# Path entries compared on GpSimd instead of rectified twice on ScalarE, and the sums of places of the alignment begun before both comparisons are done

## The reference, cut to what matters

```python
x = x + _L0_xattn_ref(ctx_1024, _layernorm(x), ...)
x = x + _L0_ffn_ref(_layernorm(x), ...)
x = x + _L1_xattn_ref(ctx_1024, _layernorm(x))     # alignment
x = x + _L1_ffn_ref(_layernorm(x), ...)            # conv block

def _align_one(small, large):                      # per sequence
    D = _pairwise_euclidean(small, large)          # 128 x 128
    R = _dtw_cost(D)                               # r = d + min(up, left, diag)
    i_idx, j_idx, valid = _backtrack(R, T_small, T_large)
    contrib = small[i_idx] * valid[:, None]
    return jnp.zeros((T_large, d)).at[j_idx].add(contrib)

def _L1_ffn_ref(x, w1, conv_w, conv_b, w2):        # bit_linear quantises x and w
    h = bit_linear(x, w1)                          # 256 -> 1024
    h = depthwise_conv1d(h, conv_w, conv_b)        # three taps over the tokens
    h = jax.nn.silu(h)
    return bit_linear(h, w2)                       # 1024 -> 256
```

## Time and profile before

| | |
|---|---|
| median of 3 runs | 3391.78 us (3389.9 to 3393.14) |
| the profiled execution | 3391.26 us, of which 3389.5 us from the first to the last instruction |
| mean granted TensorE clock | 0.956 of full speed |
| busy over the span | PE 91%, DVE 72%, ACT 53%, POOL 38% |
| the alignment's last turn (the scan waits for TensorE) to its first step back | 2888.0 to 2895.3 us |
| start of the convolution to its first hidden tile | 2957 to 2993 us |
| convolution, steps | 2993 to 3389 us |

### The profile page before, as it was taken

One profiled execution on the slowest core, in us unless ns is written; L12 is line 12 of the kernel. 1 busy time (PEld: TensorE's weight loads), 2 busy tenths in 40 slices (PEclk: granted clock), 3 DMA queues, 4 the chain that ended last, 5 costly groups with the idle time before them and its releaser, 6 DMA issues. The chain is left out here.

```text
span 3389.5 us, 63898 instructions
## 1 busy us (share of the span) xinstructions
PE 3082.9 (91%) x23092; PEld 2669.3 (79%) x23092; DVE 2443.4 (72%) x5410; ACT 1787.2 (53%) x4638; POOL 1296.7 (38%) x1194
## 2 busy tenths in 40 slices
PE   6999999999999999999998999999999953158887
PEld 5888888888888888888887888888888841046665
DVE  5666666666666666666666787878787759769998
ACT  5565655555555555555554333333333326179996
POOL 2333333333333333333332333333333320058886
PEclk9999999999999999999999999999999975589999
DMA  5000000000000000000001112121212151011101
GB/s 159 5 8 5 8 5 8 5 7 5 8 5 8 5 8 5 8 5 8 4 5 57 58 51 64 51 66 50 65 54 61 58 80 42 1 31 38 50 32 38
DMA packets 108535, 103.81 MB, mean 31 GB/s; under 512 B 26560, under 2 KB 87488, under 8 KB 108224
## 3 DMA queue, kind: packets, MB, share of 16 engines
q1 hardware_dynamic: 108224, 99.72, 10.2%
HBM read 86.55 MB, written 13.14 MB: 29 GB/s over the span
## 5 line engine op out<-in xcount | busy, mean ns | idle before, releaser
L794 POOL TENSOR_TENSOR attention_prob<-attention_prob,attention_inv_sums 128x1024 f32<-128x1024 f32 x256 | 479.6, 1894 | 399.8 <-DVE attention_inv_sums L652 399.8
L504 ACT ACTIVATE attention_prob<-attention_turns,attention_neg_max 128x256 f32<-128x256 f32 x1024 | 467.6, 482 | 175.3 <-DVE attention_neg_max L643 175.3
L1371 POOL TENSOR_TENSOR experts_hidden_lo<-experts_weighed,experts_hidden_hi 128x512 fp32r<-128x512 f32 x192 | 255.0, 1328 | 531.4 <-ACT experts_hidden_hi L1124 531.4
L659 DVE COPY attention_probT<-attention_turns 128x512 f32<-128x512 f32 x512 | 329.0, 684 | 163.1 <-PE attention_turns L380 163.0
L346 PE MATMUL attention_turns<-kv_hi,wkv 128*128 128x512 f32 x1024 | 374.1, 406 | 0.0
L643 DVE TENSOR_REDUCE attention_neg_max<-attention_turns 128x2 f32<-128x512 f32 x512 | 318.1, 684 | 45.2 <-PE attention_turns L370 44.3
L1124 ACT ACTIVATE experts_hidden_hi<-experts_weighed 128x512 fp32r<-128x512 f32 x192 | 121.4, 632 | 404.1 <-DVE experts_weighed L1261 404.1
L314 PE MATMUL attention_turns<-wkv,kv_hi 128*128 128x512 f32 x1024 | 329.8, 403 | 2.1 <-DVE kv_lo L677 2.1
L495 ACT COPY attention_v<-attention_turns 128x512 f32<-128x512 f32 x256 | 149.9, 585 | 311.1 <-PE attention_turns L314 311.1
L380 PEld LDWEIGHTS attention_turns<-ident,attention_prob 128*128 128x128 f32 x2048 | 240.0, 141 | 36.6 <-POOL attention_prob L794 3.2
L380 PE MATMUL attention_turns<-ident,attention_prob 128*128 128x128 f32 x2048 | 265.9, 273 | 2.8 <-POOL attention_prob L794 2.8
(11 more groups left out here) (287 smaller groups left out, 8948.1 us busy)
## 6 DMA issues: line engine op xcount, KB each, us to landing
experts_spread<-shares SPq DMA_DIRECT2D x256, 128.0 KB, 3.0
attention_ctx<-in_ctx SPq DMA_DIRECT2D x32, 256.0 KB, 2.7
experts_far_ctxT<-in_ctxT SPq DMA_DIRECT2D x32, 256.0 KB, 3.6
weights_ctx<-in_ctx SPq DMA_DIRECT2D x16, 512.0 KB, 3.9
out<-conv_x_out SPq DMA_DIRECT2D x15, 512.0 KB, 2.9
x_all<-in_x SPq DMA_DIRECT2D x7, 1024.0 KB, 9.2
first_x<-norms SPq DMA_DIRECT2D x16, 256.0 KB, 3.1
dist<-experts_far SPq DMA_DIRECT2D x16, 256.0 KB, 2.5
```

Source lines behind the costliest of these rows:

```text
L504: made = act.activation(prob[n % 2][:, h, :], bank_of("s", 2 * n + e)[:, m * 256:(m + 1) * 256], ACT.Exp, bias=neg_max[:, n % 2, 2 * e + m ...
L659: dve.tensor_copy(probT[n % 2][:, 2 * g:2 * g + 2].rearrange("p h t c -> p (h t c)"), bank_of("t", 2 * n + g)[:, :]).then_inc(p_copied, 1)
L794: pool.tensor_tensor(prob[n % 2][:, :, :], prob[n % 2][:, :, :], inv[:, n % 2, :].unsqueeze(2).broadcast_to([P, QH, 2 * TOK]), ALU.mult).t ...
L1371: pool.tensor_tensor(hid_lo[n % 3][:, :], weighed[n % 2], hid_hi[n % 3][:, :].bitcast(F32), ALU.subtract).then_inc(hid_split, 1)
```

## The change: the second and third pass of a path become one comparison on GpSimd, and the last turn of the alignment is reordered

Convolution. `path_gap` and ScalarE's `path_entry` are gone. GpSimd has a `path_entry` of four `tensor_scalar` comparisons (distance <= reach, 128x128 f32, per-partition scalar), at m = 4 for group g+3. Its `finish` moves from m = 1 and 3 to m = 2 and 6. `middles` makes the reach with its other sign. The first three groups' paths are made on GpSimd too, that of group 2 after the two first `inverse_std` and ahead of the steps.

Alignment. `gather` begins with the two `places` products, which wait for no comparison, then adds the `falls` of both banks (after `falls` alone is made: new semaphore `fallen`), then `left`, bank 1 first. For the last chunk the scan is cut in two, bank 1 first, and `differ` waits for each half by itself.

```diff
-                pe.wait_ge(compared, c + 1)
                 if c:
                     pe.wait_ge(scanned, c)
                 for b in range(2):
                     pe.matmul(entry_ps[:, b, :], plus[:, :], places[:, :, :].rearrange("p r j -> p (r j)"),
                               start=True, stop=False, skip_group_check=True)
-                    for weight, flags in ((minus_far, left), (minus_half, falls)):
+                for weight, flags, ready in ((minus_half, falls, fallen), (minus_far, left, compared)):
+                    pe.wait_ge(ready, c + 1)
+                    for b in reversed(range(2)):
...
             def differ(c):
-                pe.wait_ge(scanned, c + 1)
                 if c:
                     pe.wait_ge(risen, 2 * c)
                 for b in reversed(range(2)):
+                    pe.wait_ge(scanned, c + 1 + (c == CHUNKS - 1 and not b))
...
-                dve.tensor_tensor_scan(entered[:, :, :].rearrange("p r j -> p (r j)"),
-                                       goes_on[:, :, :, :].rearrange("p b r j -> p (b r j)"),
-                                       entry_ps[:, :, :].rearrange("p b n -> p (b n)"), 0.0, ALU.mult, ALU.max
-                                       ).then_inc(scanned, 1)
+                for r in (slice(0, 2 * HC),) if c < CHUNKS - 1 else (slice(HC, 2 * HC), slice(0, HC)):
+                    cols = slice(r.start * N, r.stop * N)
+                    dve.tensor_tensor_scan(entered[:, r, :].rearrange("p r j -> p (r j)"),
+                                           goes_on[:, :, :, :].rearrange("p b r j -> p (b r j)")[:, cols],
+                                           entry_ps[:, :, :].rearrange("p b n -> p (b n)")[:, cols], 0.0,
+                                           ALU.mult, ALU.max).then_inc(scanned, 1)
...
-            def path_gap(g, rows=range(GB), step=None):
-                s = g % 2
-                act.wait_ge(distance_made, g + 2 if step is None else step)
-                for i in rows:
-                    made = act.activation(gap[s][:, i, :], gap[s][:, i, :], ACT.Relu,
-                                          bias=neg_reach[:, GB * g + i:GB * g + i + 1])
-                made.then_inc(gap_made, 1)
-
-            def path_entry(g, rows=slice(0, GB), step=None):
-                s = g % 2
-                act.wait_ge(gap_made, g + 2 if step is None else step)
-                if g >= 2:
-                    act.wait_ge(expanded, 2 * (g - 1))
-                act.activation(path_sb[s][:, rows, :], gap[s][:, rows, :], ACT.Relu, scale=-4.0, bias=ones[:, 0:1]
-                               ).then_inc(path_made, 1)
...
-                if live(g + 3):
-                    if m == 0:
-                        path_distance(g + 3)
-                    if m == 2:
-                        path_gap(g + 3)
-                    if m == 4:
-                        path_entry(g + 3)
+                if m == 0 and live(g + 3):
+                    path_distance(g + 3)
...
+            def path_entry(g, rows=slice(0, GB), step=None):
+                s = g % 2
+                pool.wait_ge(distance_made, g + 2 if step is None else step)
+                if g >= 2:
+                    pool.wait_ge(expanded, 2 * (g - 1))
+                for i in range(rows.start, rows.stop):
+                    made = pool.tensor_scalar(path_sb[s][:, i, :], gap[s][:, i, :],
+                                              reach[:, GB * g + i:GB * g + i + 1], None, ALU.is_le)
+                made.then_inc(path_made, 1)
...
+            for half_ in range(2):
+                path_entry(0, slice(2 * half_, 2 * half_ + 2), half_ + 1)
+            path_entry(1)
             inverse_std(0)
             inverse_std(1)
+            path_entry(2)
...
-                if m == 1 and 0 <= g - 3 < LAST:
+                if m == 4 and live(g + 3):
+                    path_entry(g + 3)
+                if m == 2 and 0 <= g - 3 < LAST:
                     finish(g - 3, 0)
-                if m == 3 and 0 <= g - 3 < LAST:
+                if m == 6 and 0 <= g - 3 < LAST:
                     finish(g - 3, 1)
```

More of the change, by code:

```diff
@@ L1545, in gather @@
                                     weight[:, s * SEQS:(s + 1) * SEQS], flags[:, a:a + 2 * HC - 1:2, :],
-                                    start=False, stop=flags is falls, skip_group_check=True)
+                                    start=False, stop=flags is left, skip_group_check=True)
                 made.then_inc(gathered, 1)
             def differ(c):
-                pe.wait_ge(scanned, c + 1)
                 if c:
@@ L1643, in compare @@
                 dve.tensor_tensor(falls[:, f:a + LAG + 1 + CH, :], cost[:, f - 1:a + CH + LAG, 0:W],
-                                  cost[:, f - 1:a + CH + LAG, 1:], ALU.is_le)
+                                  cost[:, f - 1:a + CH + LAG, 1:], ALU.is_le).then_inc(fallen, 1)
                 if not c:
@@ L1714, in conv_ffn @@
         off_middle = st.sb("off_middle", [P, SEQS])
-        neg_reach = st.sb("neg_reach", [P, SEQS])
+        reach = st.sb("reach", [P, SEQS])
         gap = [st.sb(f"gap{i}", [P, GB, TOK]) for i in range(2)]
@@ L1750, in conv_ffn @@
         ramp_made, bounds_made, bounds_copied = st.sems("ramp_made", "bounds_made", "bounds_copied")
-        middles_made, distance_made, gap_made, path_made, expanded, x_added = st.sems(
-            "middles_made", "distance_made", "gap_made", "path_made", "expanded", "x_added")
+        middles_made, distance_made, path_made, expanded, x_added = st.sems(
+            "middles_made", "distance_made", "path_made", "expanded", "x_added")
         stats_made, rstd_made = st.sems("stats_made", "rstd_made")
@@ L1950, in path_distance @@
                     act.wait_ge(path_made, g)
+                elif not g and not rows.start:
+                    act.wait_ge(middles_made, 1)
                 for i in rows:
@@ L2036, in act_program @@
             act.wait_ge(ramp_made, 1)
-            act.wait_ge(middles_made, 1)
             for half_ in range(2):
                 path_distance(0, range(2 * half_, 2 * half_ + 2))
-                path_gap(0, range(2 * half_, 2 * half_ + 2), half_ + 1)
-                path_entry(0, slice(2 * half_, 2 * half_ + 2), half_ + 1)
             path_distance(1)
-            path_gap(1)
-            path_entry(1)
             for k in range(KD):
@@ L2049, in act_program @@
             path_distance(2)
-            path_gap(2)
-            path_entry(2)
             for n in STEPS:
@@ L2083, in middles @@
                 dve_step(dve, dve.tensor_tensor(off_middle[:, :], bounds[:, 0, :], bounds[:, 1, :], ALU.add))
-                dve.tensor_tensor(neg_reach[:, :], bounds[:, 1, :], bounds[:, 0, :], ALU.subtract)
+                dve.tensor_tensor(reach[:, :], bounds[:, 0, :], bounds[:, 1, :], ALU.subtract)
                 dve_step(dve, dve.tensor_scalar(off_middle[:, :], off_middle[:, :], -0.5, None, ALU.mult))
-                dve.tensor_scalar(neg_reach[:, :], neg_reach[:, :], 0.5, None, ALU.mult).then_inc(middles_made, 1)
+                dve.tensor_scalar(reach[:, :], reach[:, :], 0.5, None, ALU.mult).then_inc(middles_made, 1)
             def add_expanded(g, half_):
```

4 lines of the change are left out of this document (2 added, 2 removed).

## The result

The changed kernel takes 3398.78 us (median of 20 runs, 3394.68 to 3403.24), the kernel before 3392.03 beside it (20 runs, 3387.65 to 3396.82): ratio 1.0022, interval 1.0016 to 1.0028. The forecast was 3373.5, its range 3365 to 3385. The profiled execution of the changed kernel took 3402.21 us (span 3400.4), 3.4 above its median, so the traces differ by 10.9 us and the medians by 6.8.

The account below looks back on a forecast made before the run. ScalarE was taken to set the 24.08 us period, VectorE and GpSimd close behind. From 3391.26 us, 15.0 (convolution groups) and 3.2 (alignment) came off and 0.3 (convolution start) was added: 3373.4, stated as 3373.5, range 3365 to 3385.

Parts of the forecast that it names:

- ScalarE's share: Convolution: losing four `path_gap` and one `path_entry` takes 1.78 us a group off ScalarE, need 23.45 to 21.67.
- The comparison: GpSimd's 128x128 comparison in the convolution takes 0.57 us, four making 2.28 us a group; its need becomes 22.70.
- Rival 3: Convolution: a GpSimd comparison costs 1.14 us, period 25.3, time 3398.6; decides from about 0.97 us on; chance 0.07.
- Rival 2: Convolution gains nothing in full groups, ScalarE's free time becomes waits; comparisons about 0.85 us; 3385 to 3390; chance 0.08.
- The second `finish` at m = 6: Convolution, GpSimd: the moved `finish` falls where GpSimd waits for VectorE; costed at nothing, 1.28 us a group without that cover.
- Rival 1: Convolution: GpSimd or VectorE bounds near the old period, L2163 and `find_scale` lengthened; period 23.6 to 23.8, 3380.6 us; chance 0.20.
- The rule that stood beside the earlier trace: VectorE and GpSimd hold a shared SBUF port pair exclusively, the later blocks; applied to the comparisons beside L2163.
- 0.3 us of coupling: Full groups: 0.3 us added for three engines waiting on each other, instead of 0.63 before; period 23.0.
- The first groups: Start of the convolution's groups: groups 1 and 2 gain 1.5 us each, group 0 gains 1.2.
- Alignment and start: Alignment's last turn gains 3.2 us (2.1 before the scan, 1.1 from halving it); convolution's start costs 0.3 us.
- near 3410: Convolution: time if GpSimd's comparison cost 1.28 us, from about 12 cycles an element for data-dependent branching.
- The marks for "right or wrong": Right: comparison near 0.57 us, period 23.0. Wrong: comparisons over 0.75, period over 23.5, or L2163 and `find_scale` always long.

Follow-up runs that it names:

- e9: e1's kernel, paths still on ScalarE, plus four GpSimd comparisons at m = 4 that nobody reads: 3403.93 us, 13.8 above the kernel before.
- e2: Kernel before with only GpSimd's `finish` moved from m = 1 and 3 to m = 2 and 6: 3386.67 us, 3.3 below the kernel before.
- e4: Changed kernel with the second `finish` at m = 7 instead of 6: 3387.88 us, 2.0 below the kernel before.
- e3: Changed kernel with `finish` moved back to m = 1 and 3: 3399.48 us, 9.6 above the kernel before.
- e6: Changed kernel, `find_scale`'s two VectorE `tensor_scalar` made as small ScalarE passes, scale's lower bound left out: 3375.01 us, 14.1 below the kernel before.
- e7: Changed kernel with TensorE's `turn_hidden` behind expansion and output at m = 1 and 7: 3392.72 us, 3.6 above the kernel before.
- e5: Changed kernel, `finish` at m = 1 and 3, only 4 of 128 columns compared from group 3 on, output invalid: 3389.01 us, 0.1 below the kernel before.
- e1: Kernel before with the alignment part of the change alone: 3387.33 us, 2.6 below the kernel before.
- e11: e6 with e7's TensorE order: 3381.95 us, 8.2 below the kernel before.
- e12: e6 with `finish` back at m = 1 and 3: 3389.75 us, 0.4 below the kernel before.

## Why the prediction was wrong

- *ScalarE's share.* Its busy time falls from 234.54 to 222.42 us, 1.2 a group against 1.78 forecast, and it "is no longer the largest". Nothing hangs on the difference, since it waits 2.8 us a group for TensorE's output.
- *The comparison.* Right: 0.604 us against 0.57. Rival 3 (0.97 or more) is ruled out by that, although its time, 3398.6, is the one that came. Rival 2's sign came too, ScalarE's free time turned into waits, but not for its reason, comparisons of 0.85 us.
- *The step that failed: "The second `finish` at m = 6 falls where GpSimd waits for VectorE ... I cost it at nothing", and the comparisons priced as GpSimd's time alone.* Together they fill the gap in which `find_scale` ran: 1.12 us more on VectorE a group (0.170 to 1.291), and a period of 25.51, not 23.0. The comparisons weigh more: alone they cost 16.4 us (e9), while the `finish` alone costs nothing (e2). With the comparisons there, the `finish` at m = 7 has 8.8 us back (e4), at its old place nothing (e3). e6 removes what is held: its period is 23.06, where the forecast said 23.0, and it wins 14.1 us where 18.3 were forecast. The period was right for a kernel in which `find_scale` isn't held.
- *Rival 1* named this mechanism, `find_scale` meeting the `finish`, and priced it at up to 0.9 us, but took half and added it to VectorE's need only: 23.6 to 23.8. It came to 25.5: `find_scale`'s excess was 1.12 us, and TensorE's part of the loop grew as well. "Against: all those instructions but L2163 run undisturbed now" was no argument: they ran undisturbed in a gap that the change was about to fill. The rule that stood beside the earlier trace rows, the Trainium skill, "SBUF — State Buffer", section "SBUF: two separate sides", should have been laid on every place where GpSimd gets work, not on L2163's.
- *The loop left out.* The needs of three engines, each alone, and 0.3 us of coupling missed the loop between TensorE and VectorE, which had 0.8 us a group to spare. Beyond that, a us on VectorE lengthens the group, and TensorE's longer wait comes out on its clock as well: the 1.43 us a group are about half VectorE's stretch (0.76), half TensorE's (0.73). That the loop carries the loss is read from the timelines; the experiment that opens it (e7) got 3.2 us of the 15 expected, as the hold-ups grew. Nor is it shown to be why ScalarE's relief gives nothing in e5, where the `finish` stands at m = 3.
- *The first groups.* Groups 1 and 2 take 43.10 us against 43.50, 0.4 won where 3.0 was forecast; the distance from group 2 to 3 is 23.84 against 24.34. Which wait ate it was not tested. Group 0's mark is 3.6 us earlier, of which 2.2 were won ahead of it: 1.4, where 1.2 was forecast.
- *Alignment and start:* right, 3.1 us in the trace (e1: 2.6 in the median) against 3.2, and 0.2 against 0.3.
- *A figure without working.* The time "near 3410" that stands beside a comparison of 1.28 us has no sum; by the sum of rival 3 it is about 3405. Nothing hangs on it, as the comparison took 0.604 us.
- The marks for "right or wrong" did their work: comparison right, "`find_scale` long in every group" and a period over 23.5 both true.

Open: why e7's order gives its gain back in e11, beyond the wait shown, and what e12's `finish` costs besides ScalarE's 9.8 us more of waiting (15.8 against 6.0); and how e6's 21 us divide between `find_scale`, `conv_h_inv` and TensorE's clock, which all changed at once.

## What to carry to other kernels

Before you put work into an engine's idle time, look at what its neighbours do in that gap: here VectorE's smallest instructions ran while GpSimd stood idle, and filling the gap cost 9.4 us. When two engines each wait for the other once a period, add up that loop beside each engine's need, for it may have little more to spare than the engine that you relieve: here 0.8 us a group. And when a balance of loads is missed by much, look first for short instructions with long durations; rewriting two of them (e6) gave 21 us.

## What the runs showed of the hardware

- A VectorE `tensor_scalar` of 4 numbers a partition that starts beside GpSimd's `add_side`, cast or `finish` is held, and ends 0.02 to 0.03 us after one of GpSimd's instructions. Often that is the first to end: L2140 (0.88 us at 3195.72, for 0.20) ends while GpSimd's next cast, begun at 3196.52, goes on. But it can be the second or third: 1.65 us for 0.17 in e3 (addition and cast), 2.67 in the changed kernel, 2.02 in the mean in e7. The Trainium skill, "SBUF — State Buffer", section "SBUF: two separate sides", says that the later one blocks for the whole instruction of the other; by that rule 1.09 us would have been the most in e3, and the trace shows more. What decides at which end it is released is not shown.
- Not all work of GpSimd holds it: beside `inverse_std`'s power of 4 numbers (L2244, 1.04 us, from 3118.69 in the kernel before) `conv_h_inv` took 0.20 us at 3119.34.
- Beside the same GpSimd work (addition, cast, `finish`) a reciprocal of the same size took 0.178 us (e6), and the 1024-wide reduction before it 1.22: they aren't held.
- GpSimd's comparison of 128x128 with a scalar per partition took 0.603 us, one of 128x4 0.302 (e5).
- After 4.3 idle us TensorE's granted clock was 1.00 for its first products (3180.3 to 3180.9), 0.50 from 3181.5 to 3184.2 (1.2 GHz, the lower of its two levels), and 1.00 (2.4 GHz) again from 3184.6 on; the output took 3.04 us there, and 1.91 at full clock (3188.88).
